# Attention: the Fourier encoding kept in SBUF, and VectorE instead of ScalarE taking the turned queries and keys out of PSUM

## The reference

```
q, k, v = split(layernorm(x) @ w_qkv.T)              # per batch row: 256 x 16 heads x 64
fenc = fourier @ w_fproj.T + b_fproj                 # 256 x 64, the same for every head and batch row
q = q * cos + rotate_half(q) * sin + fenc
k = k * cos + rotate_half(k) * sin + fenc
attn = softmax(q @ k.T * 64 ** -0.5)
x = x + (attn @ v) @ w_out.T + b_out
```

## Time and profile before

| what | value |
|---|---|
| time, median of 3 runs | 916.82 us (915.58 to 917.76) |
| span of the profiled execution, first to last instruction | 912.4 us |
| median time less that span | 4.4 us |
| mean granted TensorE clock over the span | 0.970 |
| attention's pairs, first score to last score's start | 293.1 to 649.8 us of the span |

### The profile page before, as it was taken

How to read it: one execution, slowest core, us unless ns; L and a number is a source line. 1 busy time by engine, 2 the same in 40 slices (tenths; PEclk the granted TensorE clock), 3 DMA queues, 4 the chain that set the end, 5 groups by cost and what they waited for, 6 DMA issues and landing times.

```text
span 912.4 us, 18887 instructions
## 1 busy us (share of the span) xinstructions
PE 845.9 (93%) x6360; PEld 748.5 (82%) x6360; DVE 568.7 (62%) x1738; ACT 503.1 (55%) x1376; POOL 492.2 (54%) x536
## 2 busy tenths in 40 slices
PE   5989989999964899999999999999879999999968
PEld 4889989999963677777777777777679999999954
DVE  8947753333336877788888888877543385333337
ACT  4422333333322888888888888888732333333327
POOL 4156777777752222256666666666557254444440
PEclk9779999999996999999999999999999999999989
DMA  9947877777626890000000000000050688888648
GB/s 321 374 160 226 255 232 225 235 237 228 202 90 224 197 151 1 1 17 28 22 25 22 28 22 25 22 20 14 6 211 18 218 299 285 279 289 280 228 134 316
DMA packets 68479, 140.72 MB, mean 154 GB/s; under 512 B 10479, under 2 KB 37552, under 8 KB 68292
## 3 DMA queue, kind: packets, MB, share of 16 engines
q1 hardware_dynamic: 56644, 118.59, 40.0%
q0 software_dynamic: 11776, 21.39, 7.6%
HBM read 107.72 MB, written 35.56 MB: 157 GB/s over the span
## 4 chain that ended last, share of the span: by engine, by line
PE 51%; POOL 11%; ACT 11%; DVE 9%; issue 7%; DMA 4%; SPq 0%; DVEq 0%; ACTq 0%; POOLq 0%
PE ps L1370 12%; ACT at_prob L2255 7%; PE ps L615 7%; PE ps L1949 6%; PE ps L1389 6%; POOL y_rows L589 5%; POOL f_xg L578 5%; DVE at_nmax L2078 3%; PE ps L72 3%; PE ps L1990 2%; PE ps L655 2%; DMA f_yt<-y_rows 2%; PE ps L1975 2%; PE ps L1962 2%; ACT at_qkT L2249 2%
## 5 line engine op out<-in xcount | busy, mean ns | idle before, releaser
L1843 POOL TENSOR_TENSOR at_m<-at_m 128x512 f32<-128x512 f32 x64 | 81.4, 1272 | 146.4 <-DVE at_m L2071 146.4
L1181 POOL DMA_INDIRECT xs_rows<-xr,slots_of x128 | 127.2, 994 | 43.6 <-issue 32.0
L2255 ACT ACTIVATE at_prob<-ps,at_nmax 128x256 f32<-128x256 f32 x256 | 117.8, 474 | 39.5 <-DVE at_nmax L2078 39.0
L1350 POOL DMA_INDIRECT y_rows<-f_og,f_put x80 | 80.0, 1001 | 97.8 <-ACT f_og L1502 78.0
L878 DVE TENSOR_TENSOR f_ehid<-f_esil,ps 128x480 f32<-128x480 f32 (+1 forms) x80 | 50.7, 634 | 116.1 <-ACT f_esil L719 107.8
L1639 DVE TENSOR_TENSOR f_hid<-f_sil,ps 128x480 f32<-128x480 f32 (+1 forms) x80 | 50.6, 634 | 106.4 <-ACT f_sil L1495 99.8
L1370 PE MATMUL ps<-f_xgT,f_ring 128*128 128x160 f32 x768 | 115.0, 299 | 1.7 <-issue 1.7
L615 PE MATMUL ps<-f_xgT,f_ring 128*128 128x160 f32 x768 | 114.9, 299 | 0.2 <-issue 0.2
L719 ACT ACTIVATE f_esil<-ps 128x480 f32<-128x480 f32 (+1 forms) x80 | 44.3, 554 | 120.9 <-PE ps L615 120.9
L1495 ACT ACTIVATE f_sil<-ps 128x480 f32<-128x480 f32 (+1 forms) x80 | 44.3, 554 | 120.3 <-PE ps L1370 120.3
L1370 PEld LDWEIGHTS ps<-f_xgT,f_ring 128*128 128x128 f32 x768 | 107.0, 190 | 2.1 <-issue 2.1
(11 more groups left out here) (256 smaller groups left out, 1847.6 us busy)
## 6 DMA issues: line engine op xcount, KB each, us to landing
f_ring<-in_wexp SPq DMA_DIRECT2D x128, 576.0 KB, 5.0
y_rows<-zeros SPq DMA_DIRECT2D x16, 512.0 KB, 6.1
f_yt<-y_rows SPq DMA_DIRECT2D x16, 512.0 KB, 8.9
at_yt<-y_rows SPq DMA_DIRECT2D x6, 1024.0 KB, 4.9
xs_rows<-at_blank SPq DMA_DIRECT2D x16, 342.5 KB, 10.2
f_xg<-xs_rows SPq DMA_DIRECT2D x16, 342.5 KB, 3.4
y_rows<-f_og,f_put POOLq DMA_INDIRECT x160
y<-y_rows SPq DMA_DIRECT2D x4, 512.0 KB, 4.4
```

Of the source, the lines that this page charges most:

```text
L1181: nc.gpsimd.indirect_dma_start(xs_dram, bass.IndirectOffsetOnAxis(s.slots_of[:, t, k:k + 1], 0), s.xr[:, t, :], None, bounds_check=last_sl ...
L1843: nc.gpsimd.tensor_tensor(m1[:, p % 2, :], m1[:, p % 2, :], m2[:, p % 2, :], ALU.add).then_inc(msum, 1)
L2255: mm = nc.scalar.activation(prob[:, p % 2, h, t, :], ps[:, SB + h, t * SEQ:(t + 1) * SEQ], ACT.Exp, bias=nmax[:, p % 2, h, t:t + 1], accum ...
```

## The change

The two f32r matmuls leave `turn`. They run once, ahead of attention, into bank TB (`make_fenc`), and ScalarE copies the result into a new tile `fenc` of 128 x 512. In the loop `take_qk` moves from ScalarE to VectorE and becomes an addition: PSUM bank TB plus `fenc` into `qkT`. On VectorE it stands between `normalise(u,0)` and `invert(u,1)`, and `choice` moves behind `invert(u,1)`. `scores` gets a wait of its own on the exponentials.

```
+        fenc = sb("fenc", [P, 2 * SEQ])
...
+                def make_fenc():
+                    for half in range(2):
+                        mm = nc.tensor.matmul(ps[:, TB, half * SEQ:(half + 1) * SEQ], wfs[:, half * P:(half + 1) * P],
+                                              ffs[:, :], start=(half == 0), stop=(half == 1), skip_group_check=True)
+                    mm.then_inc(fenc_made, 1)
...
                 def turn(b, p):
...
-                    for half in range(2):
-                        mm = nc.tensor.matmul(ps[:, TB, half * SEQ:(half + 1) * SEQ], wfs[:, half * P:(half + 1) * P],
-                                              ffs[:, :], start=False, stop=(half == 1), skip_group_check=True)
                     mm.then_inc(tq, 1)
                 def scores(b, p):
                     u = PAIRS * b + p
                     pe.wait_ge(qkev, u + 1)
+                    after(pe, ex, 2 * u)
...
+                make_fenc()
                 turn_x(0, True)
...
+                pe.wait_ge(fenc_in, 1)
                 turn(0, 0)
...
+                def take_qk(b, p):
+                    u = PAIRS * b + p
+                    v.wait_ge(tq, u + 1)
+                    nc.vector.tensor_tensor(qkT[:, p % 2, :], ps[:, TB, :], fenc[:, :], ALU.add).then_inc(qkev, 1)
...
                         invert(b, p, 0)
                         normalise(b, p, 0)
+                        if there(b, p, -1, first, last):
+                            take_qk(*pair(b, p, 1))
+                        invert(b, p, 1)
                         if more:
                             choice(b + 2, p)
-                        invert(b, p, 1)
...
                 rotate(0, 1)
+                v.wait_ge(fenc_in, 1)
+                take_qk(0, 0)
                 rotate(0, 2)
...
-                def take_qk(b, p):
-                    u = PAIRS * b + p
-                    act.wait_ge(tq, u + 1)
-                    nc.scalar.copy(qkT[:, p % 2, :], ps[:, TB, :]).then_inc(qkev, 1)
...
                         exps(b, p, 1)
-                        if there(b, p, -1, first, last):
-                            take_qk(*pair(b, p, 1))
...
+                act.wait_ge(fenc_made, 1)
+                nc.scalar.copy(fenc[:, :], ps[:, TB, :]).then_inc(fenc_in, 1)
                 take_x(0)
```

More of the change, by code:

```diff
@@ L1771, in attention @@
         blank = sb("blank", [P, ROW])
+        fenc = sb("fenc", [P, 2 * SEQ])
+        fenc_made, fenc_in = sem("fenc_made"), sem("fenc_in")
         passed, passed_v = sem("passed"), sem("passed_v")
@@ L1933, in turn @@
                         for t in range(TPB):
-                            nc.tensor.matmul(ps[:, TB, half * SEQ + t * P:half * SEQ + (t + 1) * P],
+                            mm = nc.tensor.matmul(ps[:, TB, half * SEQ + t * P:half * SEQ + (t + 1) * P],
                                              m1[:, p % 2, t * QKW + half * P:t * QKW + (half + 1) * P],
-                                             ident[:, :], start=(half + t == 0), stop=False, is_transpose=True,
-                                             skip_group_check=True)
-                    for half in range(2):
-                        mm = nc.tensor.matmul(ps[:, TB, half * SEQ:(half + 1) * SEQ], wfs[:, half * P:(half + 1) * P],
-                                              ffs[:, :], start=False, stop=(half == 1), skip_group_check=True)
+                                             ident[:, :], start=(half + t == 0), stop=(half + t == TPB),
+                                             is_transpose=True, skip_group_check=True)
                     mm.then_inc(tq, 1)
@@ L2308, in _ @@
                 take_v(0, 1)
-                take_qk(0, 0)
                 take_v(0, 2)
```

## The result

The changed kernel takes 920.02 us (median; 919.07 to 920.27) against 916.2 for the kernel before (915.35 to 917.76). The medians lie 3.8 us apart. The ratio on record is 1.0049, with a 95% interval of 1.0029 to 1.0069: slower by 4.5 us, between 2.7 and 6.3. The forecast was 923.3 in a range of 915.5 to 929.0, slower.

What follows compares the result with a forecast made beforehand. The prediction took a three-engine ring to bound the pair, VectorE close behind. Its terms, 8.6 - 0.8 - 1.0 - 0.3 = +6.5 us, put the 912.4 span at 918.9; plus 4.4 gave 923.3 us, range 915.5 to 929.0.

Steps and rivals of the forecast that it cites:

- TensorE doesn't set the pace by its own work: In attention pairs: despite 98% matmul share in the middle, TensorE stands 0.23 us per pair, waiting on a three-engine ring.
- the pause at the value projection: In a plain pair TensorE could start the value projection at 455.28 but starts at 455.51, after ScalarE's `take_o`: 0.23 us.
- The size of the saving: TensorE time freed per pair when the f32r matmuls leave the loop: 0.32 us forecast.
- The ring: Pair cycle: scores, maximum, exponential, `take_qk`, `take_o`, value projection, next scores; 5.61 us, 5.15 without the 0.46 copy step.
- The price of the addition: VectorE time per added encoding: 0.605 us, bounds 0.46 and 0.685, as each instruction starts some 0.08 before the previous ends.
- the rival of the whole duration: Each VectorE addition costs 0.685 us and saves no overlap: about 929 to 930 us; chance 0.12.
- Batch rows 2 to 5: Middle attention stretch: 32 additions cost 19.4 us, less slack and overlap of 10.8, giving +8.6 us.
- Rows 0, 1, 6 and 7: Outer attention stretches: VectorE slack exceeds the additions' cost; -0.8 us taken for rows 0 and 1, -1.0 for 6 and 7.
- a surplus of 3.0: Rows 6 and 7: slack plus overlap of 12.1 us exceeds the additions' 9.1; between -3.0 and 0 expected.
- The slack of 10.8: Rows 6 and 7: VectorE's waits for TensorE ahead of maxima and rotations, 10.8 us, which additions would consume first.
- The overlap: Rows 6 and 7: each vanished VectorE wait lets its instruction overlap the previous one by 0.08 us, 16 times.
- Opening: Before the first scores: removing two f32r matmuls of 0.47 us, with the addition 0.1 dearer than the copy, gives -0.3.

## Why the prediction came out

**TensorE doesn't set the pace by its own work.** Held. Taking its f32r matmuls away gave 1 us, putting them back into the changed kernel cost 1.5 between the medians, and in both the pause at the value projection took up the difference in the pair looked at (0.23 to 0.46, and 0.97 to 0.73). The size of the saving was off: 0.25 a pair, not 0.32.

**The ring.** Held. Moving the copy out of it, with no work saved, made the kernel faster by 0.3% to 0.6%. After the change, plain pairs that VectorE doesn't set take 5.12 to 5.13 from maximum to maximum, where the sum had 5.15. How near TensorE's own work now is to the ring these runs don't settle: in the pair whose scores start at 325.95 the pause at the value projection is gone.

**The price of the addition.** 0.605 forecast; 0.60 in the timeline, and, when it was doubled, 0.59 to 0.63 in pairs where nothing else gave way. The rule that an operation starts only when the one ahead has left the pipe, and with it the rival of the whole duration, is not what these starts show. The prediction left out that the same section of the Trainium skill ("VectorE: DVE Perf Modes", "The DRAIN you can't avoid") lets a next operation that is not held start earlier, so the page does not speak for that rival.

**Batch rows 2 to 5.** Forecast +8.6, measured +7.9. VectorE waits for TensorE in them for 0.3 us in place of 9.4, as forecast. The pairs are not all of 6.0 to 6.4, as the prediction had them: five of the eight take 6.2 to 6.7, and pairs 2, 5 and 6, where VectorE had waited for TensorE, became shorter (5.43, 5.12 and 5.70). No addition waits there for the turn, and the granted clock is 1.00 (2.4 GHz).

**Rows 0, 1, 6 and 7.** I gave -0.8 to the first two and -1.0 to the last two; they gave -1.1 and -3.2. The second is the one term of the sum that was clearly mis-sized. Differences of VectorE's timelines, after less before, in us, with every idle time counted, show what made up each stretch:

| | rows 0-1 | rows 2-5 | rows 6-7 |
|---|---|---|---|
| the additions, 0.60 each | +9.6 | +19.1 | +9.0 |
| waits for TensorE | -9.4 | -8.9 | -8.6 |
| waits for exponentials | 0.0 | 0.0 | -1.0 |
| the rest, mostly starts that overlap the one before | -1.3 | -2.2 | -2.6 |
| sum | -1.1 | +7.9 | -3.2 |

For rows 6 and 7 I had held back two thirds of a surplus of 3.0, since some of VectorE's waits were single long ones in pairs that TensorE sets. That was right in kind: there it still waits 3.6 us for scores (1.1 and 0.8 of it in the last two steps, which came down from 4.64 to 4.59 and from 4.87 to 4.63). But three things were too small. The slack of 10.8 came from a window that ended just ahead of the last pair's maximum and so missed the wait of 1.3 in front of it. The overlap was put at 1.3 and came to some 2.6. And the short waits of `invert(u,1)` for the exponentials of head 1, most of the 1.0, which the addition now covers, had no place in the sum. That the result is near the whole surplus of 3.0 is luck. VectorE's waits for scores, from 567.7 to 651.0 before and from 575.2 to 655.4 after:

```profile
DVE at_nmax L2078 <- PE ps L1949: 10.1, 14, 1.8
```

```profile
DVE at_nmax L2091 <- PE ps L1955: 3.6, 5, 1.1
```

**Opening.** Forecast -0.3, measured -0.1: the first scores start 0.73 later, but GpSimd's first instruction of attention, ahead of any work that was changed, already starts 0.86 later (276.19 before, 277.05 after). That comes from the expert stage before it, where the window from 120 to 140 of the changed kernel has a granted clock of 0.91, that of the kernel before 1.00. No step of the change reaches there. From the last maximum to the end the two executions differ by another 0.5. What lowers the clock in one of two executions no run shows.

Attention by itself is thus 7.9 - 1.1 - 3.2 - 0.1 = 3.5 us longer, where I had 6.5; most of the difference is rows 6 and 7. The measured 3.8 to 4.5 us lies at the lower edge of the 4 to 9 that the prediction held most likely.

**An edit costed at nothing.** The new place of `choice` I let move back with the rest and gave no price. In the changed kernel that is right, but the addition ahead of it is what hides it: where other runs took the addition or the scaling away, it opened up. Putting it back took 0.2 to 0.7 off five of the eight pairs in rows 3 to 5, and 10 us off the time, in one of them (907.29 to 897.16).

## What to carry to other kernels

An engine that is 98% busy in modelled matmul time may still be standing in a ring; follow one period through the engines by start times, and add up the steps, before work taken off that engine is counted as time. Work that changes engines is paid where the receiving engine has no wait left for another engine, and a wait inside its own chain, like the 0.49 for the exponentials here, doesn't count as room. When an instruction is moved, ask what now covers the wait in front of it, and what happens when that cover goes.

## What the runs showed of the hardware that was not expected

In these runs GpSimd's two-input additions held up VectorE's scaling of float32 tiles in SBUF: 128x256 takes 395 ns in the mean of rows 2 to 5 before, 675 with one spare GpSimd addition a pair and 713 with one that adds the encoding, and a pair of them beside two additions took 2.42 us in place of 0.65. VectorE's tensor-tensor products from PSUM kept their 680 ns in those runs. The Trainium skill ("GPSIMD Engine Reference", section "Specifications") has GpSimd's SBUF interfaces shared with VectorE, in contention with VectorE's instructions in a two-port mode or with two SBUF inputs. That agrees for the scaling, to which the Trainium skill ("VectorE: DVE Perf Modes", section "The perf-mode tier table (the rule you actually need)") gives a 2x mode in fp32 that needs both SBUF read ports; that it is this sharing, and not another resource, no run here shows. So the additions on GpSimd, with room to spare by its own busy time, cost more than on VectorE: 929.57 (ratio 1.0166) against 920.02 (1.0049).
